# Two-layer perceiver step: the split keys take a way through HBM to the stacks, in rows of 14336 bytes

## What is computed

```
x = x + xattn0(layernorm(x), ctx)      # 16 heads of 16, softmax over 12544 positions
x = x + mamba(layernorm(x));  x = x + ffn(layernorm(x))
x = x + xattn1(layernorm(x), ctx)      # the same shape, other weights
x = x + linear_attention(layernorm(x));  x = x + sets(layernorm(x))

q = (x @ Wq + bq) per head;  k = ctx @ Wk + bk;  v = ctx @ Wv + bv
attn = softmax(q @ k.T * 16**-0.5);  out = (attn @ v) @ Wo + bo
```

## Time and profile before

| | us |
|---|---|
| median of three runs | 1390.48 |
| the profiled execution | 1387.69 |
| its span, first to last instruction | 1385.9 |
| PE busy | 1216.7 |
| DVE busy | 716.0 |
| ACT busy | 712.6 |
| POOL busy | 224.6 |
| mean granted TensorE clock, share of full speed | 0.92 |

### The profile page before, as it was taken

One profiled execution on the slowest core, in us unless ns is written; L12 is line 12 of the kernel. 1 busy time (PEld: TensorE's weight loads), 2 busy tenths in 40 slices (PEclk: granted clock), 3 DMA queues, 4 the chain that ended last, 5 costly groups with the idle time before them and its releaser, 6 DMA issues.

```text
span 1385.9 us, 29435 instructions
## 1 busy us (share of the span) xinstructions
PE 1216.7 (88%) x12725; PEld 784.6 (57%) x12725; DVE 716.0 (52%) x1348; ACT 712.6 (51%) x991; POOL 224.6 (16%) x118
## 2 busy tenths in 40 slices
PE   8799999999999988315899799999999999988556
PEld 6256666666666655315697256666566666555345
DVE  2546555555555563577222545555555555563431
ACT  3246666666666657152113256666666666657110
POOL 0222222222222200041000222222222222200000
PEclk9689999999999999558799799999999999999568
DMA  8969777777777660610706969777777777660803
GB/s 146 135 84 122 95 95 95 99 93 97 99 96 95 76 150 2 217 53 27 277 1 106 131 92 126 96 88 97 97 91 97 96 97 95 75 117 2 326 11 55
DMA packets 85155, 140.31 MB, mean 101 GB/s; under 512 B 9112, under 2 KB 76384, under 8 KB 84512
## 3 DMA queue, kind: packets, MB, share of 16 engines
q1 hardware_dynamic: 84128, 138.29, 63.9%
q10 hardware_dynamic: 896, 0.12, 0.1%
HBM read 60.05 MB, written 0.18 MB: 43 GB/s over the span
## 4 chain that ended last, share of the span: by engine, by line
PE 73%; DVE 16%; DMA 5%; issue 2%; ACT 2%; POOL 0%; SPq 0%; ACTq 0%; DVEq 0%; POOLq 0%
PE ring L547 40%; PE st L547 16%; PE ot L547 15%; DVE mpart L1202 8%; DMA qst<-rowb 3%; DVE arena L1329 2%; PE ring L678 1%; DMA arena<-scratch_perm 1%; DVE arena L1333 1%; ACT arena L921 1%; PE ring L553 0%; DMA warena<-ctxT 0%; PE ring L646 0%; DVE work L1323 0%; POOL arena L536 0%
## 5 line engine op out<-in xcount | busy, mean ns | idle before, releaser
L1202 DVE TENSOR_REDUCE mpart<-ring 128x1 f32<-128x448 f32 x896 | 516.7, 621 | 435.2 <-PE ring L547 432.8
L944 ACT ACTIVATE work<-st 128x1024 f32<-128x1024 f32 x392 | 400.8, 1022 | 197.7 <-PE st L547 193.1
L547 PE MATMUL ring<-arena,qst 96*128 96x448 bf16 x896 | 299.8, 369 | 4.9 <-DVE mpart L1202 2.7
L547 PE MATMUL st<-qst,arena 97*128 97x128 bf16 x3136 | 245.0, 221 | 19.5 <-DMA qst<-rowb 18.2
L547 PE MATMUL ot<-work,arena 128*17 128x128 f32 x6272 | 250.4, 277 | 8.9 <-issue 6.7
L547 PEld LDWEIGHTS st<-qst,arena 97*128 97x128 bf16 x3136 | 199.0, 99 | 84.3 <-issue 31.9
L547 PEld LDWEIGHTS ot<-work,arena 128*17 128x17 f32 x6272 | 138.5, 97 | 151.3 <-issue 103.7
L499 POOL TENSOR_TENSOR arena<-arena 128x896 f32<-128x896 f32 x52 | 98.2, 1888 | 715.6 <-ACT arena L917 715.6
L547 PE MATMUL ring<-warena,wkv 96*128 96x448 f32 x448 | 195.4, 566 | 2.0 <-DVE mpart L1202 1.3
L547 PE MATMUL ring<-wkv,warena 96*128 96x256 f32 x784 | 190.2, 385 | 0.9 <-DVE mpart L1202 0.8
L547 PEld LDWEIGHTS ring<-wkv,warena 96*128 96x128 f32 x784 | 147.4, 191 | 28.4 <-DVE mpart L1202 11.1
(11 more groups left out here) (269 smaller groups left out, 645.3 us busy)
## 6 DMA issues: line engine op xcount, KB each, us to landing
arena<-arena SPq DMA_DIRECT2D x336, 224.0 KB, 11.4
warena<-ctxT SPq DMA_DIRECT2D x28, 672.0 KB, 13.3
arena<-ffn_W SPq DMA_DIRECT2D x16, 1024.0 KB, 12.4
arena<-f SPq DMA_DIRECT2D x2, 4096.0 KB, 24.4
arena<-scratch_bc SPq DMA_DIRECT2D x1, 2048.0 KB, 6.7
arena<-scratch_perm SPq DMA_DIRECT2D x2, 1024.0 KB, 10.2
arena<-rows SPq DMA_DIRECT2D x1, 1792.0 KB, 7.0
warena<-w_in_proj SPq DMA_DIRECT2D x1, 1024.0 KB
```

The source lines that it names most:

```text
L547: return nc.tensor.matmul(o, l, r, start=start, stop=stop, **kw)
L944: nc.scalar.activation(pbuf[:, n % 2], st[:, 2 * (n % 2):2 * (n % 2) + 2].rearrange("p b k -> p (b k)"), ACT.Exp).then_inc(*signal(f"{lay} ...
L1202: V.reduce_max(mpart[:, 2 * h + hf:2 * h + hf + 1], ring[:, BANKS[step][0], 0:HALF], AX_X).then_inc(*signal(f"{lay}_b_max"))
```

## The change

The parts are written to a tensor in HBM, `scratch_k`, [2, 3, 128, 2, 896] in bf16, two chunks deep: six writes a chunk, in the order part 1 of m = 0 and 1, part 2, part 3, each when its part is ready. When all six have landed (`parts_out`) SP issues twelve loads from there. In HBM the two column groups of a partition lie side by side, and four consecutive partitions of the same l hold eight heads, so each load has 16 rows of 4 x 2 x 896 x 2 = 14336 bytes. The halves are now heads 0 to 7 and 8 to 15, each awaited by its own semaphore, and the b steps take the heads in order (`h, hf = n // 2, n % 2` in place of `head_of`). The wait for the buffer of the stack (s_full) stands behind the writes; the writes of a chunk wait for the loads of the chunk two before. ACT at k1 waits for the previous chunk's writes in place of its loads. Thirteen semaphores are shared by both layers instead of one for each, with the second layer's counts raised by those of the first (`of(lay, name, n)`, table `BOTH`), in the waits of all engines; one such line is shown.

```diff
+PARTS = 16 * 3 * KC
-def head_of(n):
-
-    return n // 2 % (H // KC) * KC + n // H, n % 2
+        def of(lay, name, n):
+
+            return sem(name), n + (0 if lay == "L0" else BOTH[name])
+        scratch_k = nc.dram_tensor("scratch_k", [2, 3, P, KC, CK], BF16).ap()
             def stack(lay, c):
                 b = c % KBUFS
+                if c >= 2:
+                    for half in range(2):
+                        sp.wait_ge(sem(f"{lay}_kst{half}_in"), STACK * (c - 1))
+                for part in range(3):
+                    for m in range(KC):
+                        sp.wait_ge(*of(lay, f"k{part + 1}_done", KC * c + m + 1))
+                        load(scratch_k[c % 2, part, :, m], kparts[:, part, m * CK:(m + 1) * CK], f"{lay}_parts_out")
                 if c >= KBUFS:
                     sp.wait_ge(sem(f"{lay}_s_full"), (c - KBUFS + 1) * UNITS)
-                for m in range(KC):
-                    for part in range(3):
-                        sp.wait_ge(sem(f"{lay}_k{part + 1}_done"), KC * c + m + 1)
-                        for s in range(SLOTS):
-                            if K_SPLIT[s] == part:
-                                load(kst[HD * s:HD * (s + 1), b].rearrange("l (h m) k -> l h m k", m=KC)[:, :, m],
-                                     kparts[:, part, m * CK:(m + 1) * CK], f"{lay}_kst{m}_in")
+                sp.wait_ge(sem(f"{lay}_parts_out"), PARTS * (c + 1))
+                for half in range(2):
+                    heads = slice(half * H // 2, (half + 1) * H // 2)
+                    groups = slice(half * H // 2 // KC, (half + 1) * H // 2 // KC)
+                    for s in range(SLOTS):
+                        load(kst[HD * s:HD * (s + 1), b, heads].rearrange("l h k -> l (h k)"),
+                             scratch_k[c % 2, K_SPLIT[s]].rearrange("(l g) m k -> l g (m k)", l=HD)[:, groups]
+                             .rearrange("l g n -> l (g n)"), f"{lay}_kst{half}_in")
...
-                        sp.wait_ge(sem(f"{lay}_v_full"), 4 * (c + 1))
+                        sp.wait_ge(*of(lay, "v_full", 4 * (c + 1)))
...
-                        h, hf = head_of(n)
+                        h, hf = n // 2, n % 2
...
-                        if c:
-                            act.wait_ge(sem(f"{lay}_kst{n}_in"), STACK * c)
+                        if n == 0 and c:
+                            act.wait_ge(sem(f"{lay}_parts_out"), PARTS * c)
...
-                        V.reduce_max(mpart[:, 2 * h + hf:2 * h + hf + 1], ring[:, BANKS[step][0], 0:HALF], AX_X
+                        V.reduce_max(mpart[:, n:n + 1], ring[:, BANKS[step][0], 0:HALF], AX_X
```

More of the change, by code:

```diff
@@ L161, in schedule @@
     return plan + [("o", NCH - 1, 0)]
-def head_of(n):
-    return n // 2 % (H // KC) * KC + n // H, n % 2
+BOTH = {"k1_done": KC * NCH, "k2_done": KC * NCH, "k3_done": KC * NCH, "r_done": KC * NCH, "k_full": 4 * NCH, "v_full": 4 * NCH,
+        "m_done": NCH, "mneg": NCH, "nmb": NCH, "alpha_done": NCH, "row_full": NCH, "o_full": NCH,
+        "o_scaled": NCH}
 RING_STEPS = ("row", "v", "o", "b", "k")
@@ L634, in attention @@
                                            lambda k: wkv[:, k, 1, :], None, 2)
-                        last.then_inc(*signal(f"{lay}_v_full"))
+                        last.then_inc(*signal("v_full"))
                     if kind == "b":
-                        h, hf = head_of(n)
+                        h, hf = n // 2, n % 2
                         if n % H == 0:
@@ L644, in attention @@
                     if kind == "row":
-                        pe.wait_ge(sem(f"{lay}_m_done"), c + 1)
-                        nc.tensor.transpose(ring[0:H, bank, 0:TOK], nmf[:, c % 2], ident).then_inc(*signal(f"{lay}_row_full"))
+                        pe.wait_ge(*of(lay, "m_done", c + 1))
+                        nc.tensor.transpose(ring[0:H, bank, 0:TOK], nmf[:, c % 2], ident).then_inc(*signal("row_full"))
                     if kind == "s":
@@ L678, in attention @@
                             last = nc.tensor.transpose(ring[:, bank, g * P:(g + 1) * P], ots[:, g * P:(g + 1) * P], ident)
-                        last.then_inc(*signal(f"{lay}_o_full"))
+                        last.then_inc(*signal("o_full"))
                 if lay == "L0":
@@ L907, in attention @@
                         if n == 0 and c:
-                            act.wait_ge(sem(f"{lay}_k3_done"), KC * c)
-                        act.wait_ge(sem(f"{lay}_k_full"), 4 * c + n + 1)
+                            act.wait_ge(*of(lay, "k3_done", KC * c))
+                        act.wait_ge(*of(lay, "k_full", 4 * c + n + 1))
                         nc.scalar.activation(ktf[:, m * CK + hf * HALF:m * CK + (hf + 1) * HALF],
@@ L931, in attention @@
                     if kind == "row":
-                        act.wait_ge(sem(f"{lay}_row_full"), c + 1)
+                        act.wait_ge(*of(lay, "row_full", c + 1))
                         if c:
@@ L938, in attention @@
                         act.dma_start(qst[CP:CP + 1, c % 2], rowb[:, :]).then_inc(sem(f"{lay}_row_in"), 16)
-                        nc.scalar.activation(alpha[:, c % 2], mdiff[:, :], ACT.Exp).then_inc(*signal(f"{lay}_alpha_done"))
+                        nc.scalar.activation(alpha[:, c % 2], mdiff[:, :], ACT.Exp).then_inc(*signal("alpha_done"))
                     if kind == "e":
@@ L949, in attention @@
                         if c:
-                            act.wait_ge(sem(f"{lay}_o_full"), c)
+                            act.wait_ge(*of(lay, "o_full", c))
                         nc.scalar.copy(ots[:, :], ot[:, :]).then_inc(*signal(f"{lay}_ot_out"))
@@ L1199, in attention @@
                         if n == 0 and c:
-                            dve.wait_ge(sem(f"{lay}_mneg"), c)
-                        h, hf = head_of(n)
-                        V.reduce_max(mpart[:, 2 * h + hf:2 * h + hf + 1], ring[:, BANKS[step][0], 0:HALF], AX_X
+                            dve.wait_ge(*of(lay, "mneg", c))
+                        V.reduce_max(mpart[:, n:n + 1], ring[:, BANKS[step][0], 0:HALF], AX_X
                                      ).then_inc(*signal(f"{lay}_b_max"))
```

52 lines of the change are left out of this document (26 added, 26 removed).

## The result

The changed kernel takes 1453.3 us in the median (1446.3 to 1454.6, four runs) against 1390.3 before: ratio 1.0436, 95% interval 1.0399 to 1.0474. It is slower, as forecast, and inside the range, though 23 us above the 1430 named. The profiled executions are 1452.1 and 1387.7, 64.4 us apart; the prediction's sum was 39.6.

The account below looks back on a forecast made before the run. PE, busy 88% of the span, bounds the kernel; DMA matters only where PE stands still. Starts 16.6, loops 10 and ends 13 sum to 39.6 on 1387.7: 1427.3, plus 2.8 for the median, 1430 us; range 1394 to 1466.

Parts of the forecast that it names:

- Length of row worth nothing, partitions decide: Stack reads: longer rows gain no rate; partitions written set it, so a stack still takes 22.4 us at 123 GB/s.
- 1490: Total time in us if stack loads ran at the Trainium skill's 104 GB/s, 26.5 us a stack, some 60 us more.
- Starts, forecast 16.6: Start of each layer: the second row vector lands late behind twelve reads, 8.3 us a layer, 16.6 us for two.
- (a): Layer start: six of chunk 1's reads are issued before row vector 0, which lands near 70.
- (b): Layer start, chunk 0: writes land 2.3 us after the last part is ready, and reads flow after 3.5 us.
- (c): Layer start: chunk 2's writes land at 98.3, reads flow from 99.5, row vector 1 lands at 122.3, +8.3 us.
- (d): Layer start: clock loss in PE's stands already occurs elsewhere, so no time was added for it.
- Loops, forecast 10: Loop of each layer: a write issued beside each row costs 0.5 us, over ten rows a layer, +10 us.
- Ends, forecast 13: End of each layer: the last stack drains 6.5 us later and PE's stand with it, +13 us for two.
- The first: Rival: reads from HBM are fast, from about 220 GB/s on, removing stands at starts and ends; -15, 1376 us; 16%.
- The second: Rival: reads slower still, 109 GB/s, 25.2 us a stack, delaying every loop row; 71 us in all, 1462; 14%.
- The third: Rival: only layer starts lose time, writes slip past rows, last stand does not move; 16.6 us, 1407; 20%.

Follow-up runs that it names:

- experiment 1: Two variants of the changed kernel: a copy per slot with twelve writes and 96-partition reads, 1402.1 us; 16-partition reads with rows cut to 1792 bytes, 1447.1 us.
- experiment 7: Kernel before the change, with chunk 1's loads for m = 1 held until row vector 0 has landed: 1369.7 us, ratio 0.9856.
- idle writes: Kernel before the change, stacks still loaded from SBUF, with six writes a chunk to HBM added that nobody reads: 1377.0 us, ratio 0.9916.
- experiment 2: Changed kernel with the first three chunks of each layer loaded directly from SBUF, the rest through HBM: 1410.1 us, ratio 1.0156.

## Why the prediction was right, and where its sizes were off

- *Length of row worth nothing, partitions decide.* Upheld by experiment 1, with two limits: the long row is worth some 6% of the rate, and the wide loads are larger as well. The Trainium skill, "SBUF — State Buffer", section on Door 1, ties the rate to the ports that the partitions reach: direction agrees, but its 104 GB/s, for partitions 0 to 15 and 1 MiB, is below the 123 to 135 of this queue of loads into six groups of 16, and 1490 by it would have been too high. The prediction took the advice to coalesce of the Trainium skill, "DMA: Bandwidth & Descriptors", rules for kernel authors, as speaking for the change. It does not bear on it: the advice is to merge small transfers into a large one and names those under 64 KB, while here the transfers have 224 KB before and after, and only their rows grew.
- *Starts, forecast 16.6, measured 40.0.* This is the mis-sized term. (122.3 less 114.22 is 8.1, not 8.3, so the forecast should have been 0.4 less.) Four steps of it failed. (a) "six are issued before row 0": I took 0.64 us an issue from the old loads; the reads take 5.41 / 12 = 0.45, and with the row issued 1.7 us later than worked out (62.36 for 60.7) all twelve stood ahead of it. It landed at 75.8, not near 70. (b) The last write of chunk 0 landed after 3.68 us, not 2.3, and the first reads, and row 0's issue with them, came about that much later. (c) With row 0 5.8 us later than forecast, chunk 2's reads left at 103.29 instead of 98.3, and row 1 landed at 129.3 instead of 122.3: +15.2, not +8.3. (d) "The clock falls in stands of this kind already, at another place; I add nothing for it": the second stand is a new one, and cost clock too.
- *The clock.* The stretch of 22 us behind the kernel before's wait for row 0 (the number before the DMA share is the granted clock):

```profile
68.00:90.00 22.00, 21.63 (x159) 13.66 (x159) 7.28 (x14) 10.26 (x13) 5.00 (x3) 0.77 0.36 60
```

  The same work in the held kernel of experiment 7, first up to the row, then behind it:

```profile
55.00:63.00 8.00, 8.00 (x19) 3.86 (x19) 0.00 (x0) 1.85 (x5) 0.00 (x0) 0.61 0.59 82
63.00:83.00 20.00, 19.28 (x187) 12.24 (x185) 10.25 (x19) 13.40 (x17) 6.61 (x4) 1.00 1.02 139
```

  And in the kernel with idle writes, in L0 and in L1:

```profile
64.00:84.00 20.00, 19.28 (x186) 12.23 (x183) 10.31 (x19) 13.03 (x16) 6.68 (x4) 1.00 0.67 129
...
787.00:810.00 23.00, 22.67 (x180) 14.18 (x179) 9.24 (x17) 12.11 (x15) 5.66 (x3) 0.79 0.45 87
```

  Ahead of the row the clock is partly at its lower level (1.2 GHz) in any case (0.61). Without a stand it is at 2.4 GHz from there on; after a stand of 5.25 us it is at the lower level for a part of the next 22 us. The idle writes show both in one kernel: 2.05 us in L0, then 1.00; 3.81 us in L1, then 0.79, and there row 0 to row 1 took 54.3 us, hardly less than before (54.7). So the stand of 5.25 us was worth 10.1 (57.1 less 47.0), that of 6.36 in L1 8.9 (54.7 less 45.8). The longer stand cost less clock: in L1 the 22 us behind it (799 to 821) had 0.94. The length of a stand alone does not give its price. At the change's new stand, the second, the clock falls (it was 1.00 from 105 to 124, see experiment 1):

```profile
121.00:130.00 9.00, 2.31 (x32) 1.34 (x29) 2.69 (x5) 2.05 (x4) 3.86 (x3) 0.76 0.99 203
130.00:167.00 37.00, 36.12 (x388) 22.47 (x387) 17.83 (x33) 20.96 (x26) 3.77 (x2) 0.92 0.75 126
```

  0.08 of 37 us is some 3 us in L0 (L1: 0.94 over 38 us, some 2) that the sum did not have.
- *Loops, forecast 10, measured 15.0 (8.1 to 13.1 in three other kernels with the same loop).* The size was about right, the account only in part. A write is issued just ahead of the row, and twice the writes cost the loops 14 us more. But a regular row is 0.23 us late, not 0.5; the irregular rows and the other stands carry the rest, and I had no term for them. That the sum came near is partly luck.
- *Ends, forecast 13, measured 9.4.* The last reads were issued at 504.18 and the stand at 498.83 moved to 524.55 and grew from 3.38 to 4.44 us; row 12 waited 2.99 more. The forecast passed the later drain on in full, 6.5 us a layer. The stand ended only 1.2 us later than the shift of 24.5 that L0 had brought along to row 11; with row 12's wait that is some 4 of the 6.1.
- *Rivals.* The first had its condition met in experiment 1 (above 220 GB/s), and still did not give 1376: with 231 to 260 GB/s rows 0 and 1 of L0 waited 3.5 and 2.9 us. That kernel writes twice as many bytes, so it is not quite the rival's case. The second (loads at 109 GB/s, 71 us) comes near the time and has the wrong mechanism: the rate was 134. The third, only the starts, holds two thirds of the loss; experiment 2 leaves 20 us for the rest. The sum was 23.4 us short at the starts and 5.0 in the loops, and 3.6 too high at the ends: the range was wide enough to hold that.

## What to carry to other kernels

Before making a transfer's rows longer, look at how many partitions it writes: here the rate followed that and hardly the row, and a detour through HBM bought nothing and turned "load each part when it is ready" into a barrier. A small transfer that an engine waits for was late here by what had been issued ahead of it (12.5 to 13.4 us behind twelve loads, 1.7 us alone), so the place to gain was the order of issue: hold back what is not due until the urgent one has landed, then look what stands ahead of the next one. And price a stand of the tensor engine with the clock it costs behind it, here the whole price was 40 and 90% above the stand itself.

## Not expected of the hardware

- A 4 KB transfer issued by ACT did not slip between SP's: 12.5 and 13.4 us behind twelve transfers of 224 KB. The Trainium skill, "DMA: Bandwidth & Descriptors", "Issuing engines are not separate DMA queues", says that transfers of different engines run on the same 16 DMA engines and interleave; that they share them agrees, but here interleaving did not shorten the small one's wait to anything near its 1.7 us. It was not strict order either: in the kernel before, the context load (0.69 MB) was issued at 53.46, ahead of row 0, and 0.60 MB still flowed from 68 to 71, behind the row's landing at 67.9, nearly all of it in packets longer than the 1792-byte rows of the stack loads.
- Writes to HBM added beside loads into 16 partitions ran on top of them (208 against 122 GB/s), and the kernel with 38 MB of idle writes was 0.8% faster.
- Four placements of the end of L0 (as before; last chunk's second half held; weights held as well; idle writes) show that PE's stand named "issue" follows the queued DMA: 3.38 us, none, none and none. The changed kernel has such stands at the start of each layer too, 4.52 and 4.34 us before its first score matmul, where the kernel before has none. That it is the fetch of instructions that waits is the reading that fits (each page lists DMA queues named "instruction", with about 130 packets), and not shown by a row of its own.
